# Three of the depthwise taps and the LayerNorm bias change engine, and normalised tokens are transposed in pairs

## What is computed

```python
x = x + conv_ref(_ln_c(x), ...)          # attention between channels
t = _to_tokens(x)
t = t + ffn_ref(_ln_t(t), ...)           # 4 experts, the best 2 of each token
x = _from_tokens(t, x)
# conv_ref, cut to what matters here
xn  = (x - mu) / sqrt(var + EPS_LN) * ln_w + ln_b        # over the 192 channels
qkv = einsum('bchw,oc->bohw', xn, w_qkv)                 # 192 -> 576 channels
qkv = depthwise_3x3(qkv, w_dw)                           # 9 taps for each channel
q, k, v = split(qkv * spatial_interaction)
# q, k to unit length over all pixels, softmax(q k^T) per head (24 x 24), times v, w_proj
```

## Time and profile before

| | us |
|---|---|
| median of 3 runs | 1939.6 |
| lowest and highest | 1937.39, 1943.02 |
| the profiled execution | 1935.69 |
| its span in the profile | 1933.5 |
| mean granted TensorE clock | 0.966 |

### The profile page before, as it was taken

One profiled execution on the slowest core, in us unless ns is written; L12 is line 12 of the kernel. 1 busy time (PEld: TensorE's weight loads), 2 busy tenths in 40 slices (PEclk: granted clock), 3 DMA queues, 4 the chain that ended last, 5 costly groups with the idle time before them and its releaser, 6 DMA issues. The chain is left out here.

```text
span 1933.5 us, 35208 instructions
## 1 busy us (share of the span) xinstructions
PE 1772.1 (92%) x9644; PEld 1460.3 (76%) x9644; DVE 1428.1 (74%) x3470; ACT 1253.0 (65%) x2481; POOL 1158.6 (60%) x1077
## 2 busy tenths in 40 slices
PE   5999999999987983989999999999999999999946
PEld 3666666666655773878888888888899888889934
DVE  4988999899885576778787887887866755555622
ACT  3888888888864431656666666666667666677822
POOL 3777666766661026777777777777676675444310
PEclk9999999999997986999999999999999999999977
DMA  4464533222314896878888788788787877667869
GB/s 100 148 166 130 154 96 96 86 82 81 99 38 134 269 272 219 259 197 237 247 231 237 224 249 249 198 241 225 220 219 192 251 201 199 164 178 180 236 201 335
DMA packets 246671, 364.51 MB, mean 189 GB/s; under 512 B 27620, under 2 KB 178532, under 8 KB 246436
## 3 DMA queue, kind: packets, MB, share of 16 engines
q1 hardware_dynamic: 186500, 286.26, 48.6%
q0 software_dynamic: 50016, 60.00, 15.2%
q10 hardware_dynamic: 9984, 16.26, 2.4%
HBM read 228.83 MB, written 135.73 MB: 189 GB/s over the span
## 5 line engine op out<-in xcount | busy, mean ns | idle before, releaser
L1395 POOL DMA_INDIRECT acc_scratch<-yo,tix x262 | 432.6, 1651 | 274.9 <-DVE yo L1813 168.1
L1976 PE MATMUL bank<-x_all,w1b 128*128 128x512 f32 (+1 forms) x2100 | 542.8, 388 | 1.0 <-ACT hf L1449 1.0
L1993 PE MATMUL bank<-w_hl,hh 128*128 x1572 | 491.6, 363 | 10.6 <-DVE hl L1928 6.4
L1449 ACT ACTIVATE hf<-bank,b_col 128x512 f32<-128x512 f32 (+1 forms) x420 | 277.8, 661 | 317.9 <-PE bank L1976 316.4
L1928 DVE TENSOR_TENSOR hl<-hf,hh 128x512 fp32r<-128x512 f32 (+1 forms) x420 | 274.1, 656 | 220.9 <-ACT hh L1452 219.7
L1994 PE MATMUL bank<-w_hl,hl 128*128 x1572 | 396.8, 252 | 0.0
L1976 PEld LDWEIGHTS bank<-x_all,w1b 128*128 128x128 f32 x2100 | 352.4, 188 | 49.3 <-ACT hf L1449 1.4
L666 DVE SCALAR_TENSOR_TENSOR bank<-zwin,wdw,bank 128x512 f32<-128x512 f32 (+2 forms) x462 | 336.6, 735 | 49.0 <-PE bank L766 40.4
L1380 POOL DMA_INDIRECT xs_scratch<-xn,idx x256 | 297.7, 1163 | 85.1 <-issue 75.0
L1993 PEld LDWEIGHTS bank<-w_hl,hh 128*128 128x128 f32 x1572 | 296.0, 188 | 51.0 <-issue 18.4
L1994 PEld LDWEIGHTS bank<-w_hl,hl 128*128 128x128 f32 x1572 | 299.7, 191 | 16.9
(11 more groups left out here) (267 smaller groups left out, 2901.3 us busy)
## 6 DMA issues: line engine op xcount, KB each, us to landing
w1b<-w1s_scratch SPq DMA_DIRECT2D x140, 768.0 KB, 4.9
xs<-xs_scratch SPq DMA_DIRECT2D x61, 522.0 KB, 6.0
xtok_scratch<-xtok SPq DMA_DIRECT2D x32, 384.0 KB, 2.9
xtok<-xtok_scratch SPq DMA_DIRECT2D x32, 384.0 KB, 6.9
acc_scratch<-x SPq DMA_DIRECT2D x32, 384.0 KB, 6.3
xn<-acc_scratch SPq DMA_DIRECT2D x32, 384.0 KB, 5.7
xc_a<-in_x_dram SPq DMA_DIRECT2D x32, 256.0 KB, 2.7
out_dram<-xs ACTq DMA_DIRECT2D x32, 256.0 KB, 4.7
```

The lines of the kernel that those rows point to most:

```text
L1395: nc.gpsimd.indirect_dma_start(acc_dram, bass.IndirectOffsetOnAxis(ap=tix[:, J % 4, t:t + 1], axis=0), yo[:, J % YN, t, :], None, compute_ ...
L1449: nc.scalar.activation(hf[:, k % 3, 0:cols], lb[k % 2][:, 0:cols], ACT.Gelu, bias=b1_col[:, bass.ds(exp_of[J] * CH + k, 1)]).then_inc(gelu, 1)
L1976: last = nc.tensor.matmul(lb[k % 2][:, 0:cols], w[:, q, :], v[:, J % 2, 0:cols], start=(i == 0), stop=(i == 4))
L1993: nc.tensor.matmul(out[:, 0:2 * C], hh[:, k % 3, cols], w, start=(k == 0), stop=False, skip_group_check=True)
```

## The change

- PE_TAPS of channel tile 0 loses tap 2, which VectorE takes; tiles 1 and 2 keep two taps on TensorE. VectorE has 6, 5 and 5 taps for 5, 6 and 6. ScalarE makes tap 8 of each tile as before, and tap 7 of tiles 1 and 2 as well, into more_tap. GpSimd adds more_tap to last_tap, then acc to it, then multiplies.
- xtok and tn hold two tokens' rows side by side: 128 channels of the first, the 64 last of the first, the 64 last of the second, 128 of the second. One 128x128 transpose then turns the last 64 channels of two tokens. The copy L614 goes; tp[1] gets two transposes for four. In x_c the high parts of the two tokens lie in different halves of the partitions and the low part of each in the other half, so the high copy and the subtraction are two calls each on 64x256. xtok is stored by three DMAs.
- nb is made by GpSimd, by two more links of its chain and a product, into two buffers.
- On TensorE z(i, 0) comes before dw(n, 2).

The core of the diff (widths of two constant tiles, semaphore totals and names that follow from it are left out):

```diff
-PE_TAPS = [[0, 1, 2], [0, 1], [0, 1]]
-DVE_TAPS = [[3, 4, 5, 6, 7], [2, 3, 4, 5, 6, 7], [2, 3, 4, 5, 6, 7]]
-POOL_TAP = 8
+PE_TAPS = [[0, 1], [0, 1], [0, 1]]
+DVE_TAPS = [[2, 3, 4, 5, 6, 7], [2, 3, 4, 5, 6], [2, 3, 4, 5, 6]]
+ACT_TAPS = [[8], [8, 7], [8, 7]]
+N_AT = 5
+AT_DONE = (1, 3, 5)
...
-            tn = sb(p1, "tn", [128, ROWS, 2 * 128])
-            xtok = sb(p1, "xtok", [128, 2, ROWS, C])
+            tn = sb(p1, "tn", [128, ROWS * C])
+            xtok = sb(p1, "xtok", [128, 2, ROWS * C])
...
-            nb = sb(p1, "nb", [128, ROWS])
+            nb = sb(p1, "nb", [128, 2, ROWS])
...
+            more_tap = sb(p1, "more_tap", [128, QK - 1, ROWS, W])
...
+
+            def c_part(rows, t):
+
+                return x_c[rows * CB:rows * CB + CB, 0, :].rearrange("p (a t n) -> p a t n", t=2, n=128)[:, :, t, :]
...
-                        sp.dma_start(xtok_dram[bass.ds(b.val * ROWS, ROWS), :, :].rearrange("r p c -> p r c"),
-                                     xtok[:, b.par, :, :]).then_inc(st_xt[b.par], 16)
+                        to = xtok_dram[bass.ds(b.val * ROWS, ROWS), :, :].rearrange("(a t) p c -> p t a c", t=2)
+                        pairs = xtok[:, b.par, :].rearrange("p (a n) -> p a n", a=ROWS // 2)
+                        for t, c, n, o in ((0, 0, C, 0), (1, CA, CB, C), (1, 0, CA, C + CB)):
+                            sp.dma_start(to[:, t, :, c:c + n], pairs[:, :, o:o + n]).then_inc(st_xt[b.par], 16)
...
-                links = 5
+                links = 7
...
                         for ct in range(QK):
+                            pool.wait_ge(lt_a, N_AT * n.val + AT_DONE[ct])
+                            if ct:
+                                nc.gpsimd.tensor_tensor(last_tap[:, ct, lo:hi, :], more_tap[:, ct - 1, lo:hi, :], last_tap[:, ct, lo:hi, :],
+                                                        ALU.add).then_inc(lt_p, 1)
+                                pool.wait_ge(lt_p, N_AT * n.val + AT_DONE[ct] - 1)
                             pool.wait_ge(dw_l[ct], n_dve[ct] * (n.val + 1))
-                            pool.wait_ge(lt_a, QK * n.val + ct + 1)
                             nc.gpsimd.tensor_tensor(last_tap[:, ct, lo:hi, :], acc[:, ct, lo:hi, :], last_tap[:, ct, lo:hi, :],
                                                     ALU.add).then_inc(lt_p, 1)
-                            pool.wait_ge(lt_p, QK * n.val + ct + 1)
+                            pool.wait_ge(lt_p, N_AT * n.val + AT_DONE[ct])
                             nc.gpsimd.tensor_tensor(qs[:, n.par, ct, lo:hi, :], last_tap[:, ct, lo:hi, :],
                                                     s_bc[:, n.par, lo:hi, :], ALU.mult).then_inc(qs_ok, 1)
...
                         link(5, nc.gpsimd.tensor_tensor(t[0], t[3], pw[:, 2, :], ALU.add))
+                        link(6, nc.gpsimd.tensor_tensor(t[4], mv[:, b.par, :, 0], pw[:, 3, :], ALU.mult))
+                        link(7, nc.gpsimd.tensor_tensor(t[5], t[4], t[1], ALU.mult))
                         nc.gpsimd.tensor_tensor(t[2], t[0], pw[:, 0, :], ALU.pow).then_inc(r_ok, 1)
                         pool.wait_ge(r_ok, 2 * b.val + 1)
                         nc.gpsimd.tensor_tensor(rs_all[:, bass.ds(b.val * ROWS, ROWS)], t[2], t[1], ALU.mult).then_inc(r_ok, 1)
                         pool.wait_ge(r_ok, 2 * b.val + 2)
+                        wait(pool, tn_ok, b.val - 1)
+                        nc.gpsimd.tensor_tensor(nb[:, b.par, :], t[5], t[2], ALU.mult).then_inc(nb_ok, 1)
...
                     lo, hi = slots(n)
-                    ky, kx = divmod(POOL_TAP, KX)
+                    number = ACT_TAPS[ct][k]
...
-                    nc.scalar.activation(last_tap[:, ct, lo:hi, :], zwin[n.par][:, ct, ky + lo:ky + hi, kx:kx + W], ACT.Identity,
-                                         scale=wdw[:, ct, POOL_TAP:POOL_TAP + 1]).then_inc(lt_a, 1)
+                    nc.scalar.activation(more_tap[:, ct - 1, lo:hi, :] if k else last_tap[:, ct, lo:hi, :],
+                                         zwin[n.par][:, ct, ky + lo:ky + hi, kx:kx + W], ACT.Identity,
+                                         scale=wdw[:, ct, number:number + 1]).then_inc(lt_a, 1)
...
-                        nc.scalar.activation(x_c[:, 0, :], tp[1][:, :], ACT.Copy).then_inc(hi_ok, 1)
+                        for t in (0, 1):
+                            last = nc.scalar.activation(c_part(t, t), tp[1][CB * t:CB * t + CB, 0:2 * 128].rearrange("p (a n) -> p a n", n=128), ACT.Copy)
+                        last.then_inc(hi_ok, 1)
...
-                            nc.scalar.activation(xtok[:, b.par, 2 * k:2 * k + 2, 0:CA],
+                            pair = xtok[:, b.par, 2 * k * C:2 * k * C + 2 * C]
+                            nc.scalar.activation(pair.rearrange("p (r c) -> p r c", c=CA)[:, 0:3:2, :],
                                                  tp[k][:, 0:2 * CA].rearrange("p (r c) -> p r c", c=CA), ACT.Copy)
-                            nc.scalar.activation(xtok[:, b.par, 2 * k:2 * k + 2, CA:C],
-                                                 tp[k][:, 2 * CA:2 * C].rearrange("p (r c) -> p r c", c=CB),
-                                                 ACT.Copy).then_inc(xt_a, 1)
+                            nc.scalar.activation(pair[:, CA:2 * CA], tp[k][:, 2 * CA:2 * C], ACT.Copy).then_inc(xt_a, 1)
...
                     if (i - 1).within(0, NB):
                         act.wait_ge(z_a, 5 * min(i.val, NB) if i.static else 5 * i.val)
                     tap(0)
+                    tap(1, 1)
                     if i.within(0, NB - 1):
                         copy_z(i, 0)
...
@@ -598,6 +620,7 @@
                     tap(1)
                     if i.within(0, NB - 1):
                         copy_z(i, 2)
+                    tap(2, 1)
                     tap(2)
                     if i.within(0, NB - 1):
                         copy_z(i, 3)
...
-                            last = nc.scalar.activation(tn[:, t, 0:C], xtok[:, a.par, t, 0:C], ACT.Identity, bias=nb[:, t:t + 1],
+                            last = nc.scalar.activation(tn[:, C * t:C * t + C], xtok[:, a.par, C * t:C * t + C], ACT.Identity, bias=nb[:, a.par, t:t + 1],
                                                         scale=rs_all[:, bass.ds(a.val * ROWS + t, 1)])
                         last.then_inc(tn_ok, 1)
-                        act.wait_ge(tn_ok, a.val + 1)
-                        nc.scalar.activation(tn[:, :, C:256], tn[:, :, CA:C], ACT.Copy).then_inc(tn_dup, 1)
...
-                        nc.vector.tensor_tensor(x_c[CB:128, 0, :], tp[1][CB:128, :], x_c[CB:128, 0, :].bitcast(FP32), ALU.subtract)\
-                            .then_inc(lo_ok, 1)
+                        for t in (0, 1):
+                            last = nc.vector.tensor_tensor(c_part(1 - t, t), tp[1][CB * t:CB * t + CB, 0:2 * 128].rearrange("p (a n) -> p a n", n=128),
+                                                           c_part(t, t).bitcast(FP32), ALU.subtract)
+                        last.then_inc(lo_ok, 1)
                     if has_n:
-                        tap(n, 0, HEAD_START)
+                        for k in range(HEAD_START, n_dve[0]):
+                            tap(n, 0, k)
                         for k in range(4):
                             tap(n, 1, k)
...
-                        for ct, k in ((1, 4), (2, 0), (1, 5), (2, 1), (2, 2)):
+                        for ct, k in ((2, 0), (1, 4), (2, 1), (2, 2)):
                             tap(n, ct, k)
-                    if a.within(0, NB - 1):
-                        wait(dve, tn_ok, a.val)
-                        dve.wait_ge(r_ok, 2 * a.val + 2)
-                        nc.vector.scalar_tensor_tensor(out=nb[:, :], in0=mv[:, a.par, :, 0], scalar=-1.0,
-                                                       in1=rs_all[:, bass.ds(a.val * ROWS, ROWS)], op0=ALU.mult, op1=ALU.mult).then_inc(nb_ok, 1)
-                    if has_n:
-                        tap(n, 2, 3)
                     if b.within(0, NB - 1):
                         dve.wait_ge(bn_ok, b.val + 1)
+                        wait(dve, nb_ok, b.val - 1)
                         nc.vector.memset(pause[:, 0:1], 0.0)
                         for t in range(ROWS):
                             last = nc.vector.bn_aggr(mv[:, b.par, t, :], stat[:, b.par, t, :])
                         last.then_inc(stats, 1)
                     if has_n:
+                        tap(n, 2, 3)
                         tap(n, 2, 4)
-                        tap(n, 2, 5)
...
-                        pe.wait_ge(tn_dup, i.val + 1)
+                        pe.wait_ge(tn_ok, i.val + 1)
                         wait(pe, xt_a, 2 * min(i.val + 2, NB) if i.static else 2 * i.val + 4)
-                        for h in (0, 1):
-                            for t in range(ROWS):
-                                last = nc.tensor.transpose(tp[h][:, t * 128:t * 128 + 128], tn[:, t, h * 128:h * 128 + 128], ident[:, :])
```

(13 more changed lines are left out.)

22 lines of the change are left out of this document (12 added, 10 removed).

## The result

The changed kernel takes 1945.6 us (median of 22 runs, 1939.8 to 1953.5), the one before 1941.1 (22 runs beside them, 1935.8 to 1944.7): ratio 1.0027, 95% interval 1.0017 to 1.0037. The forecast was 1941.0 in 1928 to 1952, a change of +1.4 us; the medians moved by +4.4, and the interval (some +3 to +7 us) does not take in +1.4. The profiled execution took 1949.8 us (span 1947.5, mean clock 0.962).

A forecast was written before the change was run, and what follows sets the result against it. The bound was taken as a circle of TensorE (12.26 us) and VectorE (4.50). Fill -3.1, rolled -1.3, unrolled -1.1, w1 +0.7, w2 +0.5, last four steps +4.7, last row +1.0 gave +1.4: 1941 us, range 1928 to 1952.

The forecast's parts named there:

- The GpSimd circle: First stage: from L835 through tap(1) and GpSimd's additions and products to the qs transposes and next L835; 16.65 us a step.
- the six operations: GpSimd behind tap(1): two additions and a product each for tiles 1 and 2, without a wait inside, 8.08 us.
- the last four steps: End of the first stage, from L835 to the qs transposes: 61.0 us before, 65.7 forecast by GpSimd's chain, +4.7.
- The seams of the circle: Stretches around GpSimd's six operations: 8.10 plus 0.08 us from L835 to tile 1, semaphore 0.06, three transposes 0.33.
- rival 2: GpSimd's chain longer than its parts, as tap(1) or additions come late: at 0.35 us +10, 1951; chance 0.25.
- The first circle: TensorE from L835 to the head taps, then VectorE to x_c: 16.76 us a step, forecast to go to 16.1.
- ScalarE's circle: L835 to copy_z(2) 8.27 us, tail to xh_a about 5.55, then xh_a, xl_a, x_c: 16.1 to 16.2 a step.
- GpSimd's queue in steps with pieces: GpSimd's whole work binds, or ScalarE's tail: 17.1 us with pieces of w1 (17.05 entered), 17.9 with w2.
- The fill: Start of the first stage: -1.9 us from nb's wait, the copy and transposes, -1.2 in two steps; together -3.1.
- VectorE's wait: In the changed profile VectorE would wait some 2.5 us more per step for TensorE, with nb gone.
- GpSimd keeping up: With a us more room for GpSimd's six operations, 16.1 us would rule the 17 plain steps: -15, 1925; chance 0.2.
- The clock: TensorE idle 1.1 us a step might lower its granted clock for part of the stage: 1965 us; chance 0.05.

## Why the prediction was right, and where it was not

The mechanism was right: GpSimd's chain closes the step, and the 0.8 us off TensorE come back as a wait for it. The size was low: +1.4 us forecast, +4.4 in the medians and +8.3 in the trace of the first stage, of which the load makes 4.7 and the rolled steps 2.1 (+0.8 for -1.3). That the time stayed well inside the range owes something to the range's width.

**The GpSimd circle: right.** The wait at L800 (forecast 1.1, measured 1.06), GpSimd's load (42 and 41.06 of 50), the six operations (8.08 and 293.13 to 301.18 = 8.05) and the last four steps (65.7 and 65.70) came as worked out, the last of them only in two of the four profiles of this tail (67.4 and 67.6 in the others). That the wait is the cause is shown by the run that moved tap(1): it takes nothing away and the step falls to 16.06.

**The seams of the circle: too small.** L857 to tile 1's first addition took 8.26 (8.18 forecast), product to transposes 0.14 (0.06), transposes to L857 0.38 (0.33): 16.83 instead of 16.65. This is rival 2 just under its point of 0.2 us a step, and it turned the -1.3 of the twelve rolled intervals into +0.8. The 0.06 had been VectorE's handover to TensorE (x_c to L835); GpSimd's took 0.14, twice as long.

**The first circle: right.** Forecast 16.1; 16.06 wherever it rules. Its parts: the halves of x_c take 0.86 for 0.69 on VectorE, +0.17 (forecast +0.15), and with all of the rest +0.16 in the kernel without the tap edits (forecast +0.20). The 0.05 for the z order is 0 in the rolled steps where GpSimd rules, and wasn't measured apart in rolled steps where it doesn't. ScalarE's circle, put at 16.1 to 16.2, adds up to 16.02 from the prediction's own terms (8.27, 5.55, 0.65, 0.69, 0.86), and a step with all of ScalarE's taps ran at 16.06; so it is not longer than that.

**GpSimd's queue in steps with pieces: right in kind, 0.3 too long.** GpSimd has no gap there, and the queue is the bound as said. In a step with w1, from its second small operation to the same one of the next step:

```profile
94.96 1.02 POOL L495 TENSOR_TENSOR small<-small,pw 128x4 f32<-128x4 f32 x1
...
98.98 1.98 POOL L510 TENSOR_TENSOR wpl<-stage,wph 128x384 fp32r<-128x384 f32 x2
100.92 1.28 POOL L477 TENSOR_TENSOR last_tap<-acc,last_tap 128x512 f32<-128x512 f32 x1
...
111.75 1.02 POOL L495 TENSOR_TENSOR small<-small,pw 128x4 f32<-128x4 f32 x1
```

From 94.96 to 111.75 are 16.79 us, which is the step, where 17.1 had been summed and 17.05 entered: small excesses in every term (the eight large operations 10.67 for 10.55, the small ones 4.4 for 4.3, the pieces 2.0 for 1.94). That is why those of these steps that did not wait for the load became some 0.17 us shorter than before, not longer. With pieces of w2 the steps were 17.05, 17.20 and 17.68 (17.25, 17.20 and 16.78 before).

**The load of the experts: the step that failed.** The prediction asked of each SyncE edit whether a buffer's slack is used up and answered for xtok only. It put at nothing what GpSimd's later last product does to SyncE's queue, in which s_bc waits for that product and the experts' load stands behind s_bc and four stores. The load's slack was about a us; it went out 3.2 us later in its step, 3.0 of them by GpSimd's chain, and the two steps grew by 4.7. The runs show the wait in both profiles of the changed kernel and in the kernel with only the taps, and not in those with the load first nor in the one with the three stores of xtok and the old taps.

**The fill: right in part.** -1.7 to the second turning, for -1.9. Of the -1.2 in the next two steps the second profile of the changed kernel shows all (12.44 + 13.41 = 25.85 for 27.12) and the first nothing. The first of these two steps goes with the execution: z products take 0.63 us until 40.65 in the first profile (0.39 from 41.04 on) and 0.39 from 37.85 on in the second, with a granted clock that reads 1.00 from 35 to 48 us in both; in the one profile of the kernel before it is 39.04, with 13.00 for the step, between the 12.44 and the 13.80 of the changed kernel. So what the change did in that step isn't shown. The second step is 13.4 us in both for 14.12, and the lost tap alone does not make it: with only the taps it is 14.14, with z(i, 0) put back behind dw(n, 2) 14.09, with the new order and the old taps 14.25. It takes the taps and the order together, which the term left out; its full size in one profile is in part luck.

**VectorE's wait: too large.** Forecast 2.5 us a step more; it went from 0.45 to 1.88, 1.4 more, and VectorE's busy time in the 50 us fell by 5.1, or 1.7 a step. And the row of nb's 1.30 us had no weight: in the kernel with only the taps, with GpSimd busier and nb still on VectorE, its 32 operations took 0.155 in the median and 0.59 at most.

The Trainium skill's sentence in "GPSIMD Engine Reference", Engine selection, that elementwise addition belongs on VectorE, is borne out here: with the same two taps added by GpSimd the ratio is 1.0027 (1945.6 us), with both on VectorE 0.991 (1923.2). But the version with tap(1) early keeps both on GpSimd and takes 0.9936 (1927.7). So most of that difference lies in the place in the chain, and less in the price of an addition.

The rivals: GpSimd keeping up (1925, chance 0.2) is what the kernel becomes with one line moved; the forecast's argument against it held only for the place where tap(1) stood. The clock (1965) did not fall in the rolled steps at 93% busy (1.00 in 300 to 350 us); inside the loop it was low behind the one long wait (0.59).

## What to carry to other kernels

Before a loaded engine is given more work, write down for each engine the circle from the start of a step to the operation that releases the next; an engine that is idle a third of the time can still close the longest one, and then the question is what its chain waits for at the start. An operation that needs only last step's data should not stand behind one that waits for this step's: here that place of one line was worth 18 us. And where an engine's last result comes later, follow it into the DMA queue: what waits for it there holds back every transfer behind it, also one of another purpose. Here one load, late by 2.4 us, cost 4.7 of the 8.3 us by which the stage grew.

## What the runs showed of the hardware

One wait of TensorE of 2.4 us in a stretch with 12.45 of 15 us busy was followed by 8 us at a mean granted clock of 0.59, in another execution 0.79 (between its levels of 1.2 and 2.4 GHz); the kernel with 18 VectorE taps had a wait of 2.78 us at the same place, 12.28 of 15 us busy, and kept 1.00. In both profiles of the changed kernel TensorE had also waited 1.06 us for GpSimd just before, with three transposes (0.55 us) between the two waits; in the kernel with 18 VectorE taps that earlier wait is absent. Whether that decides stays open. VectorE's taps into a bank took at most 0.758 us (median 0.756) while GpSimd was busy 41 of 50 us: nothing of GpSimd's load showed in them. They took the same in the kernel before, with GpSimd busy 32 of 50 (at most 0.757, median 0.756). GpSimd's own additions and products of 128x512 took 1.26 to 1.30 us each, six in a row.
